# Score matmuls of a packed attention stage: two 64-query halves of the array against four 32-query quarters

## The chip, the cores and the metric

The kernel runs on one core of one Trainium2 chip. The metric is device time in microseconds (us), the median of repeated executions. Times of single engines and instructions come from one further execution, taken by the hardware profiler. Engines are called as in the profile: PE is TensorE's matmul side, PEld its weight loads, DVE is VectorE, ACT is ScalarE, POOL is GpSimd, SP is SyncE.

## The reference, cut to what matters

128 sequences of 64 tokens with 128 features go through a gated cross attention with 16 heads of 8 features, and then through a mixture of 8 experts with 2 chosen per token. The part that the change touches is the score product of the attention:

```python
q = _split_heads(query @ Wq.T + bq)
k = _split_heads(key_in @ Wk.T + bk)
scores = jnp.einsum('bhqd,bhkd->bhqk', q, k) / jnp.sqrt(jnp.float32(D_K))
scores = jnp.where(pm == 0, jnp.float32(-1000000000.0), scores)
scores = scores + src_mask
p_attn = jax.nn.softmax(scores, axis=-1)
x = jnp.einsum('bhqk,bhkd->bhqd', p_attn, v)
```

Everything is float32.

## The kernel before, in words

The program has three parts that follow one another: `attention`, `experts`, `combine`. The attention stands at 29 to 504 us of the profile's span; the change is in it alone.

Attention works on 64 tiles. A tile n is 128 tokens, that is two sequences of 64. Four tiles are a quad q, and u = 0 to 3 is the tile's place in its quad. Every engine has an endless-looking list of its own: `step(j)` does eight tiles (two quads), and a loop runs steps -1 to 9, of which the middle four (j = 2 to 5) are a real loop on every engine and the others are written out. Semaphores alone order the engines.

What happens to one tile, by line of the kernel:
- PE computes the scores (`scores`, L360 to L370). The 16 heads are four groups g of four heads. The two halves h = 0, 1 of the scores take groups 2h and 2h+1 and have one PSUM bank each, `sc_ps[h]`. In a bank, partitions are the tile's 128 queries and the columns are 8 heads of 64 keys. The keys of a sequence lie in `kbd` spread block-diagonally over 4 heads (128 partitions by 256 columns), so one matmul gives four heads at once, for the queries of one sequence. The stationary operand is therefore 64 queries of `qg` wide, and a tile takes 4 groups x 2 sequences (b) = 8 matmuls. The last of each half increments `scores_done`. The first of each half waits on `masked` of the tile before, which says that DVE has read the bank.
- DVE adds the mask and moves the scores out of PSUM (`add_mask`, L535, once for each half) and takes the maximum per head (L542). POOL subtracts it (L842), ACT takes the exponent (L780), DVE sums it two tiles later (L512).
- PE turns the probabilities (L378), ACT copies them out (L775), and PE multiplies them with the values (`values`, L466). These are matmuls with a stationary operand of 32 columns, at 32g of the output partitions: four different column quarters of the array in four matmuls on end. A transpose of the spread reciprocals follows (L471).
- DVE multiplies the two (L528, `aT`), PE projects (L384), DVE adds to x (L549).
- Once a quad, PE also does transposes and projections of the next quad's inputs (L401, L405, L417, L442, L446) and the router of an earlier quad (L410, L455, L396, L426, L430). L455 also has 32-column stationary operands, four quarters on end.

PE's order in one tile is written out in `step`: scores of tile n, the quad's extra work, turn of n-2, project_out of n-4 (waits for `aT` of n-4), extra work, values of n-3. So PE's next scores come right behind the values. DVE's order is: sums of n-2 (L512), add_mask half 0, reciprocals, add_mask half 1, spread, normalise n-4 (L528), maxima, add_out, out_stats, with small steps of the two layer norms and of the routing between them.

Of the kernel before, what the change touches and what calls it, by code (L numbers as in the profile page):

```python
# [26 lines left out]
P = 128  # L27
# [5 lines left out]
S = 64  # L33
# [136 lines left out]
def attention(nc, a, NT, lists, m):  # L170
# [7 lines left out]
    with ExitStack() as ctx:  # L178
# [25 lines left out]
        qg = sb("qg", [P, 2, NG, QW])  # L204
        kbd = sb("kbd", [P, 2, QT * 2, HG, S])
# [28 lines left out]
        sc_ps, pt_ps = banks[0:2], banks[2:4]  # L234
# [29 lines left out]
        def need(eng, s, item, per=1, k=None, total=NT, apart=False):  # L264

            k = per if k is None else k
            if isinstance(item, int):
                if item < 0:
                    return
                if item >= total:  # L270
                    item, k = total - 1, per
            if apart and not isinstance(item, int):
                wait_alone(eng, s, item * per + k, passed)
            else:
                eng.wait_ge(s, item * per + k)
# [76 lines left out]
        def _(pe):  # L352
# [7 lines left out]
            def scores(n, u, par, q, h):  # L360
                if u == 0 and h == 0:
                    need(pe, q_ready, q, per=NG, total=NQ)
                    need(pe, k_ready, q, per=HG, total=NQ)
                need(pe, masked, n - 1, per=2, k=h + 1)
                for g in (2 * h, 2 * h + 1):
                    for b in range(2):
                        i = pe.matmul(sc_ps[h][b * S:(b + 1) * S, (g % 2) * 256:(g % 2) * 256 + 256],  # L367
                                      qg[:, par, g, u * P + b * S:u * P + (b + 1) * S],
                                      kbd[:, par, 2 * u + b].rearrange("p j k -> p (j k)"), start=True, stop=True)
                i.then_inc(scores_done, 1)  # L370

            def turn(n, u):
# [13 lines left out]
            def step(j):  # L386
                for v in range(2 * QT):
# [3 lines left out]
                    for h in range(2):  # L391
                        if exists(n, NT):
                            scores(n, u, par, q, h)
                        if h == 0 and u == 3 and exists(q - 2, NQ):
                            need(pe, LT_ready, q - 2, total=NQ)
                            pe.transpose(fb_ps[:, 0:P], LT[:, :], ident).then_inc(lgT_done, 1)  # L396
# [1154 lines left out]
```

## Time and profile before

| | |
|---|---|
| time before, median of 3 runs | 1036.06 us (1035.89 to 1036.55) |
| span of the profiled execution | 1026.3 us, 24733 instructions |
| PE busy | 720.7 us (70%) |
| PEld busy | 556.4 us (54%) |
| DVE busy | 771.3 us (75%) |
| ACT busy | 569.9 us (56%) |
| POOL busy | 601.1 us (59%) |

The profile gives the span of its execution, from the first to the last instruction, and no total for that execution. The median lies 9.76 us above the span. A busy time is the union of an engine's instructions, so where several matmuls overlap it is less than their count times the mean of one. "128\*64" in a matmul's row is rows by columns of the stationary operand, "128x256" is what streams through. A float32 matmul leaves two MATMUL records and two LDWEIGHTS records, a float32 transpose one.

### The profile page before, as it was taken

To read this page: it belongs to the slowest core of one execution; us is meant where nothing else is said; L and a number is where in the kernel's file an instruction comes from. 1 tells how busy PE (TensorE), PEld (TensorE's weight loads), DVE (VectorE), ACT (ScalarE), POOL (GpSimd) and SP (SyncE) were. 2 spreads that over 40 slices of the span, in tenths; PEclk is the share of its full clock that TensorE was granted. 3 is DMA by queue.
4 is the path that set the end of the run, shared out by engine and by line. 5 is a ranking of instruction groups with operands and counts; after the bars stand their busy time and mean duration, and the time that the engine had idled before them with its cause. 6 is when DMAs were issued, how large, how long until landed. Compare 5 with 4: busy or idle time off the path is not lost. (4 is left out here: it accounts for less than half of the span.)

```text
span 1026.3 us, 24733 instructions
## 1 busy us (share of the span) xinstructions
PE 720.7 (70%) x6890; PEld 556.4 (54%) x6891; DVE 771.3 (75%) x2206; ACT 569.9 (56%) x1195; POOL 601.1 (59%) x655
## 2 busy tenths in 40 slices
PE   2788778777776877887755798888998898850000
PEld 1455555454454544555435698888888887740000
DVE  5799999899898999999954975444444444436996
ACT  2767666766567666677422245555555554526553
POOL 5444466666666666666537904666666666650544
PEclk9889998989899899899856999999999999985555
DMA  4211111221112212111017201222222221215432
GB/s 119 49 37 47 42 53 44 69 59 49 52 42 68 59 50 71 42 33 33 29 45 227 68 0 53 62 59 62 62 62 62 59 62 57 62 55 149 129 117 82
DMA packets 91309, 66.22 MB, mean 65 GB/s; under 512 B 17008, under 2 KB 80752, under 8 KB 91248
## 3 DMA queue, kind: packets, MB, share of 16 engines
q1 hardware_dynamic: 70048, 35.49, 14.0%
q0 software_dynamic: 8448, 17.45, 5.4%
q10 hardware_dynamic: 12752, 12.58, 3.7%
q8 instruction: 24, 0.39, 0.2%
q14 instruction: 37, 0.30, 0.1%
HBM read 38.21 MB, written 23.09 MB: 60 GB/s over the span
## 5 line engine op out<-in xcount | busy, mean ns | idle before, releaser
L842 POOL TENSOR_TENSOR prob<-prob,mx 128x1024 f32<-128x1024 f32 x64 | 121.6, 1900 | 162.4 <-DVE mx L542 162.4
L1294 POOL DMA_INDIRECT expert_results<-y,dest x136 | 148.4, 1091 | 82.7 <-POOL dest L1290 56.2
L1108 ACT ACTIVATE hT<-bank,b1g_c,gate_c 128x256 f32<-128x256 f32 x272 | 138.3, 558 | 87.5 <-PE bank L76 87.5
L166 POOL DMA_INDIRECT expert_lists<-xn,slots x128 | 125.0, 976 | 56.9 <-issue 30.6
L1049 PE MATMUL bank<-w,hT 128*128 x1088 | 139.6, 281 | 24.1 <-ACT hT L1108 20.4
L367 PE MATMUL bank<-kbd,qg 128*64 128x256 f32 x1024 | 145.3, 427 | 6.1 <-DVE prob L535 4.9
L1049 PEld LDWEIGHTS bank<-w,hT 128*128 128x128 f32 x1088 | 127.2, 191 | 39.2 <-issue 39.2
L775 ACT ACTIVATE PT<-bank 128x512 f32<-128x512 f32 x128 | 69.2, 594 | 62.1 <-PE bank L378 62.0
L367 PEld LDWEIGHTS bank<-kbd,qg 128*64 128x64 f32 x1024 | 74.3, 152 | 52.6 <-issue 22.7
L384 PE MATMUL bank<-w_att,aT 128*128 128x128 f32 x128 | 34.2, 353 | 93.2 <-DVE aT L528 69.8
L535 DVE TENSOR_TENSOR prob<-bank,mask 128x512 f32<-128x512 f32 x128 | 86.6, 677 | 7.4 <-PE bank L367 7.1
L74 PE MATMUL bank<-rT,w_now 128*128 128x256 f32 x276 | 84.5, 306 | 7.2 <-DVE rT L68 5.0
L1211 DVE COPY meta<-rows 128x4 f32<-128x4 f32 x70 | 11.8, 170 | 101.5 <-POOL destf L1283 101.5
L512 DVE TENSOR_REDUCE sm<-prob 128x16 f32<-128x1024 f32 x64 | 77.0, 1203 | 9.3 <-ACT prob L780 9.0
L1224 DVE CAST w_now<-w 128x1024 fp32r x71 | 51.6, 727 | 37.6 <-issue 37.6
L384 PEld LDWEIGHTS bank<-w_att,aT 128*128 128x128 f32 x128 | 21.3, 209 | 105.9 <-DVE aT L528 79.6
L76 PE MATMUL bank<-rT,w_now 128*128 128x256 f32 x276 | 78.0, 283 | 0.0
L75 PE MATMUL bank<-rT,w_now 128*128 128x256 f32 x276 | 77.8, 282 | 0.0
L542 DVE TENSOR_REDUCE mx<-prob 128x16 f32<-128x1024 f32 x64 | 77.5, 1211 | 0.0
L780 ACT ACTIVATE prob<-prob 128x1024 f32<-128x1024 f32 x64 | 67.9, 1061 | 4.5 <-POOL prob L842 4.2
L378 PE MATMUL bank<-cst,prob 128*128 128x128 f32 x512 | 67.9, 277 | 0.0
L378 PEld LDWEIGHTS bank<-cst,prob 128*128 128x128 f32 x512 | 59.4, 143 | 10.0 <-issue 10.0
(183 smaller groups left out, 1751.2 us busy)
## 6 DMA issues: line engine op xcount, KB each, us to landing
rows<-expert_lists SPq DMA_DIRECT2D x70, 130.0 KB, 2.2
yin<-expert_results SPq DMA_DIRECT2D x16, 512.0 KB, 5.5
x_all<-in_x SPq DMA_DIRECT2D x16, 256.0 KB, 2.8
ctx_in<-in_ctx SPq DMA_DIRECT2D x16, 256.0 KB, 3.1
pad_k<-in_mask_BxS_ik SPq DMA_DIRECT2D x16, 256.0 KB, 4.0
xn2T<-x2T ACTq DMA_DIRECT2D x16, 256.0 KB, 2.3
out<-res ACTq DMA_DIRECT2D x7, 512.0 KB, 3.2
expert_results<-y,dest POOLq DMA_INDIRECT x136, 2.3
```

The costliest lines, as they stand in the source:

```text
L74: pe.matmul(out, ah, bh, start=True, stop=False)
L75: pe.matmul(out, ah, bl, start=False, stop=False)
L76: return pe.matmul(out, al, bh, start=False, stop=True)
L166: po.indirect_dma_start(lists[:, :], bass.IndirectOffsetOnAxis(ap=m.slots[:, par, t, k:k + 1], axis=0), m.xn2[:, par, t, :], None).then_in ...
L367: i = pe.matmul(sc_ps[h][b * S:(b + 1) * S, (g % 2) * 256:(g % 2) * 256 + 256], qg[:, par, g, u * P + b * S:u * P + (b + 1) * S], kbd[:, p ...
L378: t = pe.transpose(pt_ps[h][:, i * P:(i + 1) * P], prob[:, u, p * P:(p + 1) * P], ident)
L535: ve.tensor_tensor(prob[:, u, h * 512:(h + 1) * 512].rearrange("p (h k) -> p h k", k=S), sc_ps[h][:, :].rearrange("p (h k) -> p h k", k=S) ...
L542: ve.tensor_reduce(mx[:, u, :], prob[:, u, :].rearrange("p (h k) -> p h k", k=S), X, ALU.max).then_inc(maxed, 1)
L842: po.tensor_tensor(ps, ps, mx[:, u, :].unsqueeze(2).broadcast_to([P, H, S]), ALU.subtract).then_inc(subbed, 1)
L1049: last = pe.matmul(y_ps[par][:, h * D:(h + 1) * D], hT[:, par, c, h * P:(h + 1) * P], w2[:, bass.ds(e, 1), c, :].rearrange("p a d -> p (a ...
L1108: ac.activation(hT[:, par, c, :], h_ps[par][c // 2][:, (c % 2) * SL:(c % 2 + 1) * SL], ACT.Gelu, bias=b1g_c[:, c, bass.ds(e, 1)], scale=ga ...
L1294: po.indirect_dma_start(results[:, :], bass.IndirectOffsetOnAxis(ap=dest[:, par, h, :], axis=0), y[:, par, h, :], None).then_inc(sent[par] ...
```

## The change

In `scores`, the loop over the two 64-query halves b becomes one over four 32-query quarters r. The keys are picked by r // 2, so quarters 0 and 1 use the first sequence's keys and quarters 2 and 3 the second's. Each quarter writes its own 32 partitions of the same bank. Every score is still computed once, from the same operands. A tile's 8 matmuls become 16; the waits and the increments stay, the increment on the last matmul of each half.

```diff
                 for g in (2 * h, 2 * h + 1):
-                    for b in range(2):
-                        i = pe.matmul(sc_ps[h][b * S:(b + 1) * S, (g % 2) * 256:(g % 2) * 256 + 256],
-                                      qg[:, par, g, u * P + b * S:u * P + (b + 1) * S],
-                                      kbd[:, par, 2 * u + b].rearrange("p j k -> p (j k)"), start=True, stop=True)
+                    for r in range(4):
+                        i = pe.matmul(sc_ps[h][32 * r:32 * r + 32, (g % 2) * 256:(g % 2) * 256 + 256],
+                                      qg[:, par, g, u * P + 32 * r:u * P + 32 * r + 32],
+                                      kbd[:, par, 2 * u + r // 2].rearrange("p j k -> p (j k)"),
+                                      start=True, stop=True)
                 i.then_inc(scores_done, 1)
```

## Rows read from the trace of the kernel before

**Rows 1.** Busy time in two of three whole passes of the attention's loop.
```profile
core 0: us, PE busy (x) PEld busy (x) DVE busy (x) ACT busy (x) POOL busy (x), PEclk, DMA share, GB/s
197.20:261.00 63.80, 47.33 (x579) 31.51 (x571) 60.16 (x177) 42.12 (x83) 40.67 (x32) 0.92 0.20 54
261.00:324.80 63.80, 47.95 (x575) 31.63 (x567) 59.77 (x177) 41.97 (x83) 40.68 (x32) 0.92 0.21 54
```

**Rows 2.** DVE's waits in the three passes (197 to 389): total, times, longest.
```profile
DVE sm L512 <- ACT prob L780: 8.5, 3, 2.9
DVE prob L535 <- PE bank L367: 1.0, 3, 0.4
```

**Rows 3.** PE's waits in the same stretch, with the same columns.
```profile
PE bank L384 <- DVE aT L528: 32.8, 18, 5.6
PE bank L384 <- issue: 9.7, 6, 3.2
```

**Rows 4.** Groups of the attention, 29 to 504: busy, mean ns, idle before.
```profile
L367 PE MATMUL bank<-kbd,qg 128*64 128x256 f32 x1022 | 144.9, 426 | 6.1 <-DVE prob L535 4.9 <-ACT kbd L805 0.9 <-issue 0.2
...
L535 DVE TENSOR_TENSOR prob<-bank,mask 128x512 f32<-128x512 f32 x127 | 85.9, 677 | 7.1 <-PE bank L367 6.8
```

**Rows 5.** PE in order of time, 414.00 to 414.03: the burst's first two score records.
```profile
414.00 0.44 PE L367 MATMUL bank<-kbd,qg 128*64 128x256 f32 x2
```

**Rows 6.** PE in order of time, 279 to 287: one tile at full clock.
```profile
281.16 0.65 PE L466 MATMUL bank<-PT,vb 128*32 128x64 f32 x32
...
282.00 1.95 PE L367 MATMUL bank<-kbd,qg 128*64 128x256 f32 x16
...
285.36 1.04 PE L378 MATMUL bank<-cst,prob 128*128 128x128 f32 x8
```

**Rows 7.** Score records of the whole run: ns min/median/max.
```profile
L367 PEld LDWEIGHTS bank<-kbd,qg x1024: 132/137/232, 28.9 to 503.9; 128*64 128x64 f32 x171
L367 PE MATMUL bank<-kbd,qg x1024: 379/379/690, 29.0 to 504.3; 128*64 128x256 f32 x171
```

**Rows 8.** The same for the two lines with 32-column stationary operands, 29 to 504.
```profile
L466 PE MATMUL bank<-PT,vb x1920: 219/219/317, 46.4 to 500.2; 128*32 128x64 f32 x192
...
L455 PEld LDWEIGHTS bank<-x2T,router x112: 106/108/109, 99.7 to 500.6; 128*32 128x32 f32 x112
L455 PE MATMUL bank<-x2T,router x112: 272/285/297, 99.7 to 500.7; 128*32 128x128 f32 x112
```

**Rows 9.** PE at 413.64 to 413.70: the first four L455 records; then 413.70 to 413.82.
```profile
413.65 0.32 PE L455 MATMUL bank<-x2T,router 128*32 128x128 f32 x4
...
413.65 0.43 PE L455 MATMUL bank<-x2T,router 128*32 128x128 f32 x8
```

**Rows 10.** PE in order of time, 268 to 279: a tile after a long idle.
```profile
271.13 0.80 PE L384 MATMUL bank<-w_att,aT 128*128 128x128 f32 x2 [5.48 <-DVE aT L528]
...
274.13 2.85 PE L367 MATMUL bank<-kbd,qg 128*64 128x256 f32 x16
...
272.00:275.00 3.00, 3.00 (x41) 1.94 (x41) 3.00 (x6) 0.88 (x2) 2.64 (x2) 0.50 0.01 3
```

**Rows 11.** DVE in order of time, 271 to 278: the wait for those scores.
```profile
276.15 0.69 DVE L535 TENSOR_TENSOR prob<-bank,mask 128x512 f32<-128x512 f32 x1 [0.37 <-PE bank L367]
```

**Rows 12.** DVE, then PE, around the jump back to the loop's start (261 us).
```profile
264.17 0.29 DVE L554 BATCH_NORM_STATS2 st<-x_all 128x6 f32 x1
267.25 1.22 DVE L512 TENSOR_REDUCE sm<-prob 128x16 f32<-128x1024 f32 x1 [2.79 <-ACT prob L780]
...
261.65 1.95 PE L367 MATMUL bank<-kbd,qg 128*64 128x256 f32 x16
```

**Rows 13.** Instruction queues' packets, MB, share: 40 to 192 us, then 192 to 389.
```profile
q8 instruction: 12, 0.20, 0.5%
...
q10 hardware_dynamic: 1008, 1.84, 2.5%
q14 instruction: 17, 0.14, 0.3%
```

## The prediction

> **What bounds the kernel now.** I read the table of busy times first, for the shares, but it averages over three parts with different limits, and the edit lies in the attention alone. So the second view is the busy time of each engine in single passes of the attention's real loop. A pass is eight tiles and takes 63.8 us. The reader is to see that DVE is busy for 59.8 to 60.2 us of it and PE for 47.3 to 48.0 [rows 1]. DVE sets the pace, at 7.98 us a tile, and PE has 16 us a pass, 2.0 us a tile, in which it does nothing. The third view is what each of the two waits for. DVE's largest waits in three passes are for something else than the scores: 8.5 us in 3 times, once at each jump back, against 1.0 us in 3 times for the scores [rows 2]. PE's are the other way round: 32.8 us of 192 for DVE's `aT`, and 9.7 us with no releaser shown ("issue") at the same line [rows 3]. Over the whole attention DVE waited 6.8 us for score matmuls, out of 475 [rows 4]. So an edit of the score matmuls reaches the end time only through those few waits, unless it makes PE slower by more than its cover.
>
> **Does the array already run the two halves together?** This decides what there is to gain. Two score records start within 0.01 us: together they take 0.44 us, and one lasts 0.379 to 0.43 [rows 5, 7]. Sixteen records take 1.95 us [rows 6]. If they go in eight pairs, the pairs are (1.95 - 0.379) / 7 = 0.224 us apart. For comparison, L378 sends 128 columns through the full width, eight records in 1.04 us [rows 6]; with a tail of 0.28 us, as L455 has for the same 128 columns [rows 8], that is (1.04 - 0.28) / 7 = 0.109 us for each, so 256 columns cost 0.218 us. A pair of halves costs one pass of 256 columns, not two. The array is full already; quarters can fill it no better.
>
> **Do four quarters run together?** The trace has two lines with 32-column stationary operands. L466 does 32 records of 64 columns in 0.65 us with a tail of 0.219 [rows 6, 8]: in waves of four that is (0.65 - 0.219) / 7 = 0.062 us a wave, against 64/128 x 0.109 = 0.054 us for one pass. L455's first four records are all under way within 0.32 us, where one lasts up to 0.297, and all eight are through after 0.43 [rows 8, 9]. So four quarters share a pass at 64 and at 128 columns, and they start (0.32 - 0.297) / 3 = 0.008 us apart. No row shows it at 256 columns; the rows at hand are one and two doublings away and show no loss that grows with the length.
>
> **The change part by part.**
> - Matmul records: a tile had 4 groups x 2 halves x 2 records = 16 in 8 pairs. It will have 32 in 8 waves of four, each wave still 256 columns of streaming. Stream time per tile: 8 passes before, 8 passes after, difference 0. If quarters went only two at a time it would be 16 passes, +8 x 0.216 = +1.73 us a tile (0.216 being 0.224 less the first load's share, below). These are the two ends; I take the first, by the L455 and L466 rows.
> - Starts: the last record of a wave starts 3 x 0.008 after the first, not 1 x 0.008: +0.015 us on the end of each half.
> - Weight loads: 16 records of 64 columns, 0.137 us each, become 32 of 32 columns at 0.108 us [rows 7, 8]. Four on end need 0.108 + 0.024 = 0.13 us, below the 0.22 us of the wave that hides them. Only a burst's first loads lie open: a first pair's record takes 0.43 us against 0.379, so 0.05 us; in L455 it is 0.297 against 0.273, so 0.024 [rows 5, 7, 8]. That gives back 0.027 us a burst. With the line above the net is -0.012 us; I bound it by -0.03 and +0.03 and take 0.
> - PE's issue: a burst has 64 instructions in place of 32, to be handed over in about 1.6 us, 0.025 us each. In L466 the same engine took 64 (32 records, 32 loads) in 0.65 - 0.219 = 0.43 us, 0.007 us each [rows 6, 8]. Cost nothing, hidden by the streaming.
> - What follows a score burst on PE, and the waits on `masked`, are as before; DVE, ACT and POOL get no instruction more or less, and no DMA is added but instruction fetch. The increment on `scores_done` comes with the last quarter, inside the +0.015 us.
> - Where it counts: in the loop DVE waits once a pass of 64 us for the scores, 0.3 to 0.4 us, in the tile that follows PE's idle of 5.48 us, where the granted clock is 0.50 (1.2 GHz) and the burst takes 2.85 us [rows 2, 10, 11]. Every ns there is a ns of the end time. Even at one such wait per quad, 16 x 0.03 = 0.5 us either way; at the value taken, 16 x -0.012 = -0.2 us, which I call 0.
>
> Sum against the profiled execution: 1026.3 + 0 = 1026.3 us span. The median of the runs is 9.76 us above that span, and nothing of the edit lies outside it, so 1036.1 us.
>
> **A page's figure that speaks against this.** The rows above show four quarters sharing a pass with 0.062 us for 0.054 us of streaming. The Trainium skill (TensorE: Matmul & The Clock Gate, Part 3, Measured speedup vs the span model) gives three column tiles of 32 at 512 columns a speedup of 2.38, short of 3, though it models a wave as one matmul plus 4 ns a tile; here the starts are 8 ns apart. By its 2.38 a wave would be longer by 3 / 2.38 = 1.26, a tile's burst by 8 x 0.216 x 0.26 = 0.45 us, and that is the milder form of the first rival.
>
> **The rivals.**
> 1. Quarters don't fully share at 256 columns, so PE becomes the bound (slower). Price at the far end: 8 tiles x 1.73 = 13.8 us a pass on top of 47.8 gives 61.6 us of PE work in a 63.8 us pass [rows 1]. It fits on paper, but PE's waits for `aT` [rows 3] are spread unevenly, and the tile in which DVE waits already gets all of it. From one full burst a quad, 16 x 1.73 = 28 us, up to one in each of 64 tiles, 110 us: 1064 to 1147 us, and I would say 1075. In the mild form, +0.45 us a tile, the 2.0 us of idle cover most tiles and one wait a quad takes it: 16 x 0.45 = 7, so 1036 to 1043. Against it: rows 8 and 9. It decides from about 0.3 us more per burst in the tile of rows 11, since 0.37 us are waited there already. Chance 0.05 for both.
> 2. The longer loop body costs PE a refetch at the jump back (slower). DVE shows what that looks like: after the last line of a pass it starts the first of the next 2.79 us later [rows 12], three times in three passes [rows 2], though ACT's exponent that the row names lies behind it. PE pays nothing there now: its scores come at 261.65, right after the jump [rows 12], and one instruction queue that moves 12 packets while the steps are written out moves none in the loop [rows 13], so I read it as PE's and its body as resident. The body has (575 + 567) = 1142 records [rows 1] and gets 8 x 32 = 256 more. If it no longer fits, three jumps cost PE 2.8 us each. That lies beside DVE's own stall: scores 2.8 us later would still be there by 266.5, and DVE asks for them after L512, which ends at 268.5 [rows 12]. So 0 us by the rows, at most 3 x 2.8 = 8.4 us: 1036 to 1044.5. Chance that it costs over 0.2%: 0.02. The Trainium skill (Runtime: NRT & Kernel Launch, Instruction fetch mechanics) gives PE's buffer as 2048 instructions, by which the longer body fits; the missing queue in the loop agrees.
> 3. Shorter exposed loads, and the same column split of the array in L455 and in the scores of u = 3, get the scores out earlier (faster). L455's eight records take two waves, 0.11 us apart (0.43 - 0.32, rows 9), and the scores start 0.35 us after its first [rows 5, 9], so at most 0.35 - 0.22 = 0.13 us lie in the change of split, once a quad: 16 x 0.13 = 2.1 us if every one were on the path. DVE's waits were in another tile [rows 10, 11], so it isn't. All waits for scores together are the 6.8 us of rows 4, most of it in the first tiles. Time 1035.6 by the 0.5 us above, 1034.0 if the 2.1 us counted. Chance of over 0.2% faster: 0.03. The Trainium skill (TensorEngine Tiling (Array Packing), Key Properties) says that changing the tiling mode drains TensorE; the 0.13 us is the most that the rows leave for it.
>
> **How the numbers follow.** 0.2% of 1036 is 2.1 us, about what a measurement of this kernel can tell from no change. The forecast case, no change by the array being full and DVE setting the pace: 0.90, its own range 1035.2 to 1037.0 (0.5 us for the wait terms and the spread of the runs shown). Faster 0.03 from rival 3; slower 0.07 from rivals 1 and 2. For 8 in 10 I take 1034.8 to 1038.0.
>
> **What would show it.** Right: MATMUL records of the score line 2048, in one tile 32 of them in 1.94 to 1.98 us at full clock; loads of 0.108 us; PE busy per pass within 0.3 us of 47.8; DVE's waits for the scores still about 1 us in three passes; the passes 63.8 us. Wrong: a burst above 2.2 us at full clock (rival 1), fetches in the loop on the queue that was silent and a gap of 2 to 3 us on PE at 197, 261 and 325 us (rival 2), DVE's waits at L535 gone (rival 3). The forecast fails if the time of a pass moves though none of these does, say through a different course of the granted clock.

## The result, and the profile after

The change made the kernel slower by 0.7% where it was timed: 1043.48 us (1037.52 to 1046.39, six runs) against 1035.94 us (1031.69 to 1036.55, six runs of the kernel before, timed beside it), a ratio of 1.0069 with a 95% interval of 1.0047 to 1.0092. The forecast was 1036.1 us and "no change"; the time lies above its range of 1034.8 to 1038.0.

The page of the kernel after: the span, busy times and the two groups that answer to [rows 4].

```profile
span 1044.2 us, 26781 instructions
...
PE 717.5 (69%) x7914; PEld 546.5 (52%) x7915; DVE 771.6 (74%) x2206; ACT 570.1 (55%) x1195; POOL 599.7 (57%) x655
...
L367 PE MATMUL bank<-kbd,qg 128*32 128x256 f32 x2048 | 140.3, 414 | 6.9 <-DVE prob L536 4.3
...
L536 DVE TENSOR_TENSOR prob<-bank,mask 128x512 f32<-128x512 f32 x128 | 86.6, 677 | 14.0 <-PE bank L367 9.3
```

No engine has more to do: PE 717.5 us against 720.7, DVE 771.6 against 771.3. What grew is DVE's idle time ahead of the mask addition (L536 now, L535 before): 14.0 us against 7.1. Two passes of the loop, to be held against [rows 1], and DVE's waits of the three passes, to be held against [rows 2] (total, times, longest):

```profile
199.80:265.40 65.60, 48.22 (x697) 30.76 (x689) 59.90 (x177) 42.17 (x83) 40.62 (x32) 0.92 0.19 53
265.40:329.50 64.10, 47.94 (x697) 30.63 (x689) 59.87 (x177) 42.29 (x83) 40.62 (x32) 0.92 0.21 54
```
```profile
DVE sm L513 <- issue: 8.6, 3, 3.0
DVE prob L536 <- PE bank L367: 2.8, 6, 1.4
DVE prob L536 <- remote: 1.4, 1, 1.4
```

One pass is 1.8 us longer, the other 0.3 us, with DVE's busy time as before, PE's 0.9 us up in the first and level in the second, and the same granted clock of 0.92. The last line has a releaser that the trace of the kernel before doesn't have at all: "remote", the profile's word where it shows no sender on this core. At that place the trace shows the wait and the burst it waited for. DVE, then PE, in order of time, kernel after:

```profile
252.44 1.19 DVE L513 TENSOR_REDUCE sm<-prob 128x16 f32<-128x1024 f32 x1
253.73 0.69 DVE L536 TENSOR_TENSOR prob<-bank,mask 128x512 f32<-128x512 f32 x1
254.34 0.24 DVE L518 RECIPROCAL sm<-sm 128x16 f32<-128x16 f32 x1
255.96 0.69 DVE L536 TENSOR_TENSOR prob<-bank,mask 128x512 f32<-128x512 f32 x1 [1.38 <-remote]
```
```profile
252.28 2.14 PE L367 MATMUL bank<-kbd,qg 128*32 128x256 f32 x32
254.35 0.66 PE L411 MATMUL bank<-cst,xn 128*128 128x128 f32 x4
254.84 1.04 PE L379 MATMUL bank<-cst,prob 128*128 128x128 f32 x8
257.70 0.49 PE L385 MATMUL bank<-w_att,aT 128*128 128x128 f32 x2 [1.82 <-DVE aT L529]
```

The scores are through at 252.28 + 2.14 = 254.42, DVE is free from 254.6 on, and it starts at 255.96, when PE has just run out of work (254.84 + 1.04 = 255.88). The score records came in time; the increment of `scores_done` that DVE waits for, called the signal from here on, did not. So two things want an explanation: why the signal was late, and whether the quarters are to blame for it.

### The profile page after: what moved, and what is told of

The parts are those of the page before. It is cut to its first block and busy times, and to the rows that moved or that the text cites. A ratio compares the mean times of both kernels' runs of the same rounds, so it can differ in the third digit from the quotient of the medians.

```text
span 1044.2 us, 26781 instructions
## 1 busy us (share of the span) xinstructions
PE 717.5 (69%) x7914; PEld 546.5 (52%) x7915; DVE 771.6 (74%) x2206; ACT 570.1 (55%) x1195; POOL 599.7 (57%) x655
## 5 line engine op out<-in xcount | busy, mean ns | idle before, releaser
L367 PE MATMUL bank<-kbd,qg 128*32 128x256 f32 x2048 | 140.3, 414 | 6.9 <-DVE prob L536 4.3
L385 PE MATMUL bank<-w_att,aT 128*128 128x128 f32 x128 | 34.0, 351 | 99.6 <-DVE aT L529 59.8
L536 DVE TENSOR_TENSOR prob<-bank,mask 128x512 f32<-128x512 f32 x128 | 86.6, 677 | 14.0 <-PE bank L367 9.3
L367 PEld LDWEIGHTS bank<-kbd,qg 128*32 128x32 f32 x2048 | 64.2, 118 | 55.7 <-issue 22.2
```

The source lines that it names most:

```text
L367: i = pe.matmul(sc_ps[h][32 * r:32 * r + 32, (g % 2) * 256:(g % 2) * 256 + 256], qg[:, par, g, u * P + 32 * r:u * P + 32 * r + 32], kbd[:, ...
L536: ve.tensor_tensor(prob[:, u, h * 512:(h + 1) * 512].rearrange("p (h k) -> p h k", k=S), sc_ps[h][:, :].rearrange("p (h k) -> p h k", k=S) ...
```

## The experiments

In this section a **stretch** is the time from the start of the mask addition of tile 12 to that of tile 61 (it is there 128 times, two per tile, so from the 25th record to the 123rd). It leaves out the first and the last tiles. It is 379.9 us in the trace of the kernel before and 389.7 us in that of the kernel after. It is taken from traces, so from one execution each. In all edits `r`, `h`, `g`, `u` are those of the diff above, and the increments stay on the last matmul of each half. The ratios in the tables compare a kernel with the kernel before as it ran beside it on the same chip.

**First set: is it the quarters, or the number of PE instructions?** Halves with the keys in two pieces (a1) have as many records as the quarters but no 32-column operand; four pieces (a2) double them again.

```diff
+                    for s in range(2):        # a1; a2: range(4), pieces of 64 columns
                     for b in range(2):
-                        ... (g % 2) * 256:(g % 2) * 256 + 256 ..., kbd[:, par, 2 * u + b]
+                        ... (g % 2) * 256 + s * 128:(g % 2) * 256 + (s + 1) * 128 ..., kbd[:, par, 2 * u + b, s * 2:(s + 1) * 2]
```

> Each half's matmul is cut along the 256 key columns into two of 128; the stationary operand stays 64 queries wide. A tile has 16 score matmuls as the changed kernel has, 64 score records on PE where before has 32. Theory count (what costs is the number of PE instructions: behind the array something takes them at a bounded mean rate, about 44 ns each, read from 8474 PE instructions in 373.4 us of the changed kernel's attention): slower than before like the changed kernel, 1042 to 1046 us, and DVE waits at L535 for scores whose last record ended over 1 us earlier. Theory quarters (what costs is the 32-column split itself): no change, within 2 us of before.

> Halves as before, keys cut into four pieces of 64 columns: 32 score matmuls a tile, 128 score records. Theory count: about 152 - 32 + 128 = 248 PE instructions a tile, x 44 ns = 10.9 us a tile against 7.98, so 64 x 2.9 = +187 us: about 1220 us, though PE's recorded busy time stays below 52 us per 64 us of the loop before. Theory quarters: no change in the score bursts but for some 0.01 us a piece, 1036 to 1042. The loop body grows by 768 PE instructions here, so a refetch at the three jumps back (up to 8.4 us) may be added under either.

a3 keeps the quarters and takes half of the value product away, a4 has quarters in one half of the scores:

```diff
-                    for c in range(2):                 # values, a3
+                    for c in range(1):
```
```diff
-                    for r in range(4):                 # scores, a4
+                    for r in range(4) if h == 1 else (0, 2):   # 32 queries wide, or 64
```

> The changed kernel, and of the values' product only the matmuls with c = 0 (8 of 16 a tile) are done, so half of the value product is left out. PE has 32 instructions a tile fewer, as many as before has; the score quarters are all there. Theory count: the loss is gone, 1036 us or below (DVE sets the pace again). Theory quarters: 1042 to 1046, since PE had room for the left-out 0.25 us a tile anyway.

> Quarters in score half 1 only, halves in score half 0: half of the change. 168 PE instructions a tile. Theory count: 168 x 44 ns = 7.4 us a tile, below DVE's 7.98, so the mean rate is no bound: within 2 us of before. Theory quarters: about half of the 7.5 us, 1039 to 1040.

| run | score records of a tile | us | ratio to before (95%) | stretch |
|---|---|---|---|---|
| before, same chip | 16 | 1036.7 | | |
| a1 | 32, halves | 1047.3 | 1.0094 (1.0060 to 1.0128) | 393.7 |
| a2 | 64, halves | 1090.06 | 1.0528 (1.0501 to 1.0555) | 428.1 |
| a3 | 32, quarters | 1049.14 | 1.0119 (1.0102 to 1.0136) | 388.0 |
| a4 | 24, both | 1044.22 | 1.0087 (1.0053 to 1.0121) | 386.7 |

a1 is the clearest: with no quarter anywhere it loses as much as the change does. So rival 1, quarters that don't share a pass, is not the cause. The theory that I put against it, one mean time for each instruction that PE issues, was to give about 187 us in a2; it gave 53. a4 should have lost nothing by it and lost all; a3 has as many PE instructions a tile as the kernel before (152) and still lost. It fell. (With half of the values missing the tokens are routed differently, and the experts' part runs one step more. That is about 8 us: on a chip of the next set, what follows the last mask addition takes 527.9 us in c4 and 519.9 in c1. a3 less 8 us is still 4 us above its kernel before. Its stretch, which that step doesn't touch, is 388.0 us against 379.9.)

**The two kernels again, on two other chips.**

> The kernel before, unchanged, for a trace of an execution as slow as its timed runs (their spans were 1034 to 1036 us, the trace shown has 1026.3). Theory late signals (PE's signals come up to 2 us after its records' end in the changed kernel, and cost DVE the time): the kernel before has fewer of them than the changed kernel in the attention, under 3 us of DVE's waits, and the rest of the 8 us between 1026 and 1035 lies behind 530 us. Theory drift of the base: the kernel before shows the same late signals in the attention, and the comparison of the two shown traces overstates the edit.

> The changed kernel, unchanged, beside the kernel before on one chip. Ratio 1.004 to 1.009 again. Theory late signals: its attention is 4 to 7 us longer than that of the kernel before in the trace of the same chip, all of it in DVE's waits at L536.

> The kernel before, unchanged. On one chip it took 1024.5 us and ran its attention without late signals, on others 1035 to 1037. Theory late signals: where it takes 1035 or more, its own trace shows PE's signals over 1 us after the end of the record that gives them, in the attention or behind it at 530 to 550 us; where it takes 1025, it shows none.

> The changed kernel, unchanged. Theory late signals: level with c1_before (within 1 us) on a chip where c1_before takes 1025 us, 5 to 9 us above it where c1_before takes 1035, the excess in DVE's waits at L536. Theory edit (the edit costs PE or the array something of its own): the same excess on every chip, which the 1.0004 measured once already speaks against.

> 64-query halves with the keys in four pieces of 64 columns, 128 score records a tile. It took 53 us more on one chip. Theory late signals: where c1_before takes 1025 us this takes 1025 to 1030, since PE's recorded work hardly grows; where c1_before takes 1035 it takes about 1090 again. Theory PE bound (the 96 further records a tile cost PE real time): 50 us more on any chip.

> The changed kernel with half of the value product left out (c = 1), as many PE instructions a tile as before. Other routing follows from that, and with it one more step of the experts' list (about 8.6 us, to be taken off). Less that: level with c1_before wherever it runs, by theory count (late signals go with the number of PE instructions); at c2_quarters by theory quarters.

| run | us | ratio (95%) | stretch |
|---|---|---|---|
| b1, before | 1023.96 | 0.9994 (0.9976 to 1.0012) | 379.7 |
| b2, quarters | 1025.14 | 1.0004 (0.9993 to 1.0014) | 379.7 |
| c1, before | 1025.1 | 1.0020 (1.0003 to 1.0038) | 379.0 |
| c2, quarters | 1023.48 | 0.9990 (0.9975 to 1.0004) | 379.1 |
| c3, as a2 | 1033.13 | 1.0080 (1.0053 to 1.0107) | 386.4 |
| c4, as a3 | 1031.45 | 1.0077 (1.0050 to 1.0104), 8 us of it the further step | |

I had expected the loss to repeat, and it was gone. On these two chips the kernel before takes 1024 us, 12 us less than before, and the quarters cost nothing. (c1 is the kernel before held against itself, and its interval still leaves out 1, so differences of 0.2% are not to be read.) Loop passes of c2, one tile's score burst at full clock, and DVE's waits in the three passes (195 to 395):

```profile
199.60:263.60 64.00, 47.26 (x688) 30.39 (x688) 59.93 (x176) 41.91 (x83) 40.63 (x33) 0.92 0.20 54
263.60:327.70 64.10, 47.66 (x688) 30.51 (x688) 59.91 (x176) 41.90 (x83) 40.64 (x33) 0.92 0.21 54
```
```profile
279.91 1.93 PE L367 MATMUL bank<-kbd,qg 128*32 128x256 f32 x32
```
```profile
DVE sm L513 <- ACT prob L781: 8.7, 3, 3.0
DVE prob L536 <- PE bank L367: 2.3, 6, 0.6
```

32 records of 32 columns take 1.93 us where 16 of 64 took 1.95 [rows 6]: four quarters cost one pass of 256 columns. That is the array's side of the forecast, confirmed.

c3 took 1033 us where I had expected 1025 to 1030, and is far from the 50 us more that the further records were to cost if they took PE real time. It shows something else, cleanly, since here no signals are late: what happens when the loop's body grows too long. It is the kernel of a2. PE in order of time after the jump back, PE's wait there, a pass, and the instruction queues of the loop (packets, MB, share); the last fence is the only instruction queue that c2 has in the same stretch.

```profile
262.06 0.33 PE L473 MATMUL bank<-cst,rsx 128*128 128x128 f32 x1
269.17 1.55 PE L368 MATMUL bank<-kbd,qg 128*64 128x64 f32 x24 [6.78 <-issue]
```
```profile
PE bank L368 <- issue: 20.3, 3, 6.8
```
```profile
202.50:269.10 66.60, 51.47 (x944) 42.88 (x944) 59.46 (x177) 41.66 (x82) 40.62 (x32) 0.86 0.20 55
```
```profile
q8 instruction: 30, 0.49, 1.1%
q14 instruction: 16, 0.13, 0.2%
```
```profile
q14 instruction: 17, 0.14, 0.3%
```

q8, silent in the loop before [rows 13] and silent in c2, moves 30 packets in three passes; PE stands for 6.78 us after each jump; the pass is 66.6 us and not 64.0. So a refetch costs PE 6.8 us and the kernel about 2.5 us a jump (386.4 - 379.0 = 7.4 us in three); the rest, as I read it, lies beside DVE's own stall of 2.8 us and in PE's slack. That the 7.4 us are the jumps' and not the shorter pieces' shows where they fall: from tile 20 to tile 44, across the three jumps, c3 takes 199.3 us and c1 191.8; over the other tiles of the stretch, with the same pieces, both take 187.2 us. This is rival 2, real, but not for this edit: 688 + 688 = 1376 recorded instructions a pass stay resident, 944 + 944 = 1888 do not. The Trainium skill (Runtime: NRT & Kernel Launch, Instruction fetch mechanics) gives PE's buffer as 2048 instructions. The 1376 agree with it; the 1888 do so only if PE executes some 160 more a pass than are recorded, which no run here shows.

**The kernel before and after on a chip of the first kind.** d1 and d2 are the two kernels, d3 the kernel before with half of the value product left out, d4 quarters and two key pieces together (64 records a tile, as a2).

> The kernel before, unchanged. Theory base: if it takes 1035 us or more here, its own trace shows late signals of PE and waits of DVE at L535 or behind the attention that the 1025 us traces do not have. If it takes 1025 us: none.

> The changed kernel, unchanged. Level with d1_before where that takes 1025 us (third chip), 5 to 9 us above it where that takes 1035 or more.

> The kernel before with half of the value product left out (c = 1): 120 PE instructions a tile for 152. One more step of the experts' list follows (8.6 us, to be taken off). Theory count (late signals go with the number of PE instructions): where d1_before takes 1035 us or more this, less 8.6, is 3 us or more below it; where it takes 1025, within 1.5 us. Theory site (late signals do not depend on PE's number of instructions): level with d1_before everywhere.

> 32-query quarters with the keys in two pieces of 128 columns: 32 score matmuls a tile, 128 score records, as many as the halves with four pieces had. Theory refetch (that kernel's 8 to 9 us on the undisturbed chip are PE's stop at the three jumps back, once the loop's body has 768 instructions more): 1032 to 1034 us on a chip where d1_before takes 1025, with waits at L535 right behind the three jumps. Theory short pieces (64 columns were too short for the array): 1025 to 1027. Where d1_before takes 1035: about 1090, as the halves with four pieces, by theory count.

| run | us | ratio (95%) | stretch |
|---|---|---|---|
| d1, before | 1037.8 | 1.0009 (0.9997 to 1.0021) | 379.8 |
| d2, quarters | 1051.74 | 1.0127 (1.0094 to 1.0160) | 395.4 |
| d3, before less values | 1039.4 | 1.0032 (1.0019 to 1.0044), 8 us of it the further step | 378.1 |
| d4, quarters and 2 pieces | 1089.4 | 1.0499 (1.0474 to 1.0524) | 437.3 |

On this chip the loss is back, and with 13.9 us (1051.74 - 1037.8) larger than the 5 to 9 us that I had expected; d4 came out at the expected 1090. And d1, which is the kernel before, holds the cause of the chips' own difference. ACT and PE in order of time behind the last tiles, first c1 (a 1024 us chip), then d1 (a 1036 us chip):

```profile
517.06 0.42 PE L455 MATMUL bank<-x2T,router 128*32 128x128 f32 x8
...
517.55 0.37 ACT L799 ACTIVATE LT<-bank,router 128x128 f32<-128x128 f32 x1 [0.95 <-PE bank L455]
```
```profile
520.77 0.43 PE L455 MATMUL bank<-x2T,router 128*32 128x128 f32 x8
...
530.05 0.37 ACT L799 ACTIVATE LT<-bank,router 128x128 f32<-128x128 f32 x1 [9.74 <-remote]
...
530.47 0.47 PE L396 MATMUL bank<-cst,LT 128*128 128x128 f32 x1 [9.27 <-ACT LT L799]
```

In c1 ACT starts 0.07 us after L455's last record, in d1 8.85 us after it, with PE, ACT and DVE all idle in between. A second such place follows in the experts' part. DVE's longest wait there, c1, then d1:

```profile
DVE xn2T L1128 <- PE bank L1005: 15.8, 11, 10.7
```
```profile
DVE xn2T L1128 <- remote: 17.2, 1, 17.2
```

8.8 us here and 17.2 - 10.7 = 6.5 us there, 15.3 together, are about as much as the part behind the last mask addition is longer (534.3 us in d1, 519.9 in c1, 14.4 more). The spans are 1038.8 and 1021.0 us. The word "remote" marks the chips (it stands for a signal that came over 1.5 us after the record that gave it, too late for the profile to see the two together): it stands in the waits of all nine traces from chips where the kernel before takes 1036 us, and in none from the others. Nor does it stand in the trace of rows 1 to 13. And the edit's loss is of the same kind. PE and DVE of d2 (quarters):

```profile
328.69 1.62 PE L367 MATMUL bank<-kbd,qg 128*32 128x256 f32 x16
330.25 1.16 PE L418 MATMUL bank<-w_att,cT 128*128 128x128 f32 x8
331.24 1.04 PE L379 MATMUL bank<-cst,prob 128*128 128x128 f32 x8
```
```profile
330.26 0.19 DVE L619 TENSOR_REDUCE r_m<-ra 128x4 f32<-128x32 f32 x1
332.41 0.69 DVE L536 TENSOR_TENSOR prob<-bank,mask 128x512 f32<-128x512 f32 x1 [1.96 <-remote]
```

The second half's scores end at 330.31, DVE waits until 332.41, and PE's last record before it ends at 332.28. Such waits grow with the score records. DVE's waits with this releaser in the whole trace: the kernel after, a1, d2, a2, d4, in this order (d1, d3, a3 and a4 have none at this line):

```profile
DVE prob L536 <- remote: 3.0, 2, 1.6
```
```profile
DVE prob L537 <- remote: 3.3, 2, 1.8
```
```profile
DVE prob L536 <- remote: 9.9, 6, 2.1
```
```profile
DVE prob L537 <- remote: 41.4, 23, 2.9
```
```profile
DVE prob L537 <- remote: 51.4, 29, 3.1
```

Shorter delays stand under PE's own name, so the word alone counts too little. Counted from the records themselves, for each mask addition of the stretch: from the end of the score record that it awaits, or of DVE's instruction before it if that is later, to its start, where this is over 0.2 us. In the traces with 16 score records a tile and in all from the 1024 us chips (before, d1 and d3; b, c, e and f) there is no such case. The others, beside what their stretch is longer than that of the kernel before (379.9, a2's than c3's 386.4, which is the same kernel):

| trace | score records of a tile | late starts | sum, us | longest, us | stretch longer by, us |
|---|---|---|---|---|---|
| a4 | 24 | 6 | 4.4 | 1.0 | 6.8 |
| a3 | 32 | 8 | 6.5 | 1.1 | 8.1 |
| after | 32 | 6 | 6.9 | 1.6 | 9.8 |
| a1 | 32 | 9 | 10.9 | 1.8 | 13.8 |
| d2 | 32 | 10 | 14.2 | 2.1 | 15.5 |
| a2 | 64 | 24 | 39.9 | 2.9 | 41.7 |
| d4 | 64 | 27 | 46.9 | 3.1 | 57.4, with the refetch |

So late signals make up two thirds to nearly all of what each of these kernels loses in the stretch. d3 has fewer records than the kernel before, and less the 8 us of the further step it is at 1031.4 against 1035.9, as the theory of a count had it; but its stretch is only 1.7 us shorter than d1's, and most of the gain is its wait at L799, 3.8 us where d1's was 9.7.

**Is it the number in one burst, or in all?** a3 and d1 say something on this already: with 152 PE instructions a tile both, a3 has late starts and a longer stretch (388.0 us against 379.8), so the number in all doesn't decide alone. e1 and f1 put the further records in the value product and leave the scores in halves; e2 has quarters in half 0 only.

```diff
+                    for w in range(2):                 # values, e1 and f1
                     for c in range(2):
                         for g in range(NG):
-                            ... att_ps[..., b * S:(b + 1) * S] ..., PT[..., p * P + b * S:p * P + (b + 1) * S]
+                            ... att_ps[..., b * S + 32 * w:b * S + 32 * w + 32] ..., PT[..., p * P + b * S + 32 * w:p * P + b * S + 32 * w + 32]
```

> Scores as before (halves, 32 records a tile); each value matmul is cut into two of 32 query columns, so the values have 64 records a tile for 32, 216 PE instructions a tile for 152 (the quarters have 184). Where the kernel before takes 1035 us or more: by theory burst (what makes the scores' signal late is the number of records in the score burst itself) level with before, attention 380 to 382 us for tiles 12 to 61; by theory total (all PE instructions count alike) slower than the quarters, 1050 to 1060. Where it takes 1025: level by both, within 2 us.

> Quarters in score half 0, halves in half 1 (the other one-half version had it the other way round and took 0.9% more on such a chip). Where the kernel before takes 1035 us or more: by theory burst the whole burst counts, not which half, 1042 to 1048; if only the records right ahead of the second signal counted, level with before. Where it takes 1025: level.

> The kernel with 64 value records a tile and halves in the scores again, for a chip where the kernel before takes 1035 us or more. There: theory burst 1034 to 1040 us and no large waits of DVE at L535 in the attention; theory total 1050 to 1060. Where the kernel before takes 1025: level again, nothing told apart.

> The changed kernel beside it on the same chip: 5 to 14 us above the kernel before where that takes 1035 us or more, level where it takes 1025 (a fourth such chip).

| run | us | ratio (95%) | stretch |
|---|---|---|---|
| e1 | 1023.78 | 1.0001 (0.9984 to 1.0019) | 379.7 |
| e2 | 1023.64 | 1.0002 (0.9988 to 1.0016) | 379.0 |
| f1 | 1024.54 | 1.0005 (0.9991 to 1.0019) | 379.7 |
| f2, quarters | 1024.39 | 1.0003 (0.9986 to 1.0020) | 378.3 |

The e set ran on the chip of b, the f set on another where the kernel before takes 1024 us, and there nothing shows, as f2 tells: the control lost nothing either. They make it three such chips on which the quarters are level. Whether further records outside the score burst would cost anything on a 1036 us chip stays open.

**What stays open.** Why the signals come late on some chips, and whether the recording of the execution has a part in it, since every run here was also recorded. The traces of the 1036 us chips lack about a quarter of the semaphore changes that the others hold (some 9,700 against 12,900), though no instruction (24733 in d1 as in c1), so there the recording itself is short of something. Both begin at one place: in the first 120 us d1 has 1145 changes and c1 1152, from 125 to 300 us 1585 and 2202, and the first signal that is over 0.1 us late comes at 124 to 136 us in each of the nine traces. The Trainium skill (NOTIFIC — the notification-queue block, 7.1 Overflow) says that the block which writes such records holds back inside itself rather than lose one, and that this can throttle an engine. That would fit a loss that grows with PE's records, though holding back doesn't explain records that are missing; no run here shows that block, and I leave it as a candidate. A run that is timed without being recorded would tell, and there is none.

## Why the prediction was wrong, by its own steps

- **The array is full, four quarters share a pass: right.** 1.93 us for a tile's 32 records, under the 1.94 to 1.98 forecast.
- **Starts, loads, PE's issue, net -0.012 us a burst taken as 0: right** on three chips, where the ratio was 1.0004, 0.9990 and 1.0003. The records are 2048 as forecast, and a load's median is 0.110 us for the 0.108 forecast; PE's busy time in a pass, forecast within 0.3 us of 47.8, was 47.26 and 47.66 in c2.
- **DVE sets the pace: right.** 59.9 us of a pass in c2 and in the kernel after, 59.8 to 60.2 in [rows 1].
- **The failed step: "the increment on `scores_done` comes with the last quarter, inside the +0.015 us".** I equated the signal with the end of the record. In the trace of rows 1 to 13 it holds: none of the 518 signals of PE in its first 520 us comes over 0.045 us after the end of its record. Where the change was timed it doesn't: DVE started 1.5 us after the end of the score records in the kernel after, 2.1 us in d2. The loss grows with the number of records in the score burst (a1, a2, d4), and that is what the change doubled. The term that I set to 0 was worth 1043.48 - 1035.94 = 7.5 us there, and 1051.74 - 1037.8 = 13.9 us in d2. Why the signals are late on such a chip stays open, as said above.
- **The hint that I read over: the 9.76 us between span and median.** I took it as a fixed part outside the span. It is not: the profiled execution of the kernel after took 1046.1 us with a span of 1044.2, so 1.9 us lie outside, and in every other run on record it is 1.8 to 2.4. By that a span of 1026.3 belongs to a time of 1028.2, and the 1036 of the runs was already another condition than the one traced. Its trace has none of the marks of the 1036 us chips either: no "remote", and 12,926 semaphore changes. The rows could not speak for the runs, and the range had to be wider. It also means that the 17.9 us between the two spans shown (1026.3 and 1044.2) are not all the edit's: 7.7 us are that condition (1035.94 - 1028.2), 7.5 us the edit, and by 2.6 us the profiled execution lies above its median (1046.1 - 1043.48).
- **Rival 1** fell by a1 and c2. **Rival 2** is a real mechanism, but not at this length: the kernel after has no q8 packet from 195 to 395 us, and that 1043.48 lies inside this rival's range is chance. So is it that its price in c3 (7.4 us for three jumps) is near my "at most 8.4": PE stands for 6.8 us a jump, where I had 2.8 from DVE's row, and 2.5 of them reach the end time, where I had 0. **Rival 3**: no gain is seen; DVE's waits for the scores stayed.
- **The Trainium skill's figure of 2.38** (TensorE: Matmul & The Clock Gate, Part 3) for three column tiles, which by my reading would have made a burst 0.45 us longer, is not what these rows show: the burst of four tiles was 0.02 us shorter than that of the halves.
- The closing sentence of the forecast, that it fails if a pass moves though none of the listed marks does, is near to what happened. None of the marks of the rivals came; of those of "right", DVE's waits for the scores missed theirs (2.8 + 1.4 us in three passes for about 1), and through them, not through the granted clock (0.92 in both), the pass moved.

## What to carry to other kernels

Compare the span of the profiled execution with the time of the runs before anything else: if they differ by more than the kernel's own start and end, the trace doesn't show what was timed, and a forecast from it needs room for that. More and smaller matmuls that fill the array equally well are level by the array and can still lose on some chips by the number of records in the burst that another engine awaits, so test a change of that kind on more than one chip and put the kernel before beside it each time. In the trace, hold the end of the awaited record against the start of the one that waits: where they are a microsecond or more apart and the waiting engine stands, it is the signal that came late and not the work.

## What the runs showed of the hardware that I had not expected

- The same program takes 1024 us on some chips (three here) and 1036 us on others, with the granted clock at 0.882 to 0.887 on both (d1, c1).
- On the latter, signals from PE arrive late: DVE's start by up to 2.1 us in the attention with 32 score records a tile and up to 3.1 us with 64, ACT's by 8.85 us once behind it. The semaphore changes in the traces say the same. In the first 520 us of the eleven undisturbed traces each of PE's, some 520, comes 13 to 56 ns after its record's end. In the nine others 48 to 118 of some 490 come over 0.1 us late, the longest 2.5 us in the kernel after and 3.7 us in d4, and often in a row, 59 or 60 ns apart. The first one over 0.5 us comes at 125.6 us in the kernel after and at 135.8 us in d1. So the kernel before has them too (52 of 485), but its attention isn't longer for it (379.8 us).
- What it costs rises steeply with PE's records in the score burst of a tile, each against the kernel before on such a chip: 24 to 32 records 0.7 to 1.3%, 64 records 5.0 to 5.3%, of which by c3 0.8% is the refetch.
- A loop body of 1888 recorded PE instructions is fetched again at each jump (c3): 6.78 us in which PE does nothing, against none at 1376 (c2).
